# Decoder layer on one core: a piece of the weight maximum placed between VectorE's reciprocal and the context scaling

## The reference

```python
def bitlinear(x, w):
    xq = _act_quant(_rmsnorm(x))
    wq = _weight_quant(w)
    return jnp.einsum('bsd,ed->bse', xq, wq)
...
scores = jnp.einsum('bshd,bstd->bsht', q, k) / Dh ** 0.5
attn = jax.nn.softmax(scores, axis=-1)
ctx = jnp.einsum('bsht,bstd->bshd', attn, v)
ctx = jnp.swapaxes(ctx, 1, 2).reshape(B, S, D)
return bitlinear(ctx, wo)
...
o = jnp.einsum('bsef,edf->bsed', h, W2) + b2
```

## Time and profile before

| | us |
|---|---|
| median of 3 runs | 783.32 (782.77 to 783.34) |
| the profiled execution, its time | 779.51 |
| its span | 777.8 |
| VectorE busy in the span | 573.6 (74%) |
| TensorE busy (matmuls) | 626.6 (81%) |
| ScalarE, GpSimd busy | 488.9, 492.7 (63% each) |
| the loop of self-attention slots | from 67.8 to 215.2 |

### The profile page before, as it was taken

The page is one execution under the profiler, slowest core; times in us unless marked ns, Lnnn a source line. Parts: engine busy times, 40 slices in busy tenths (PEclk is TensorE's granted clock), DMA queues, the critical chain, the costliest instruction groups (busy, mean ns, idle before and its releaser), DMA issues.

```text
span 777.8 us, 20249 instructions
## 1 busy us (share of the span) xinstructions
PE 626.6 (81%) x6601; PEld 544.6 (70%) x6601; DVE 573.6 (74%) x1717; ACT 488.9 (63%) x994; POOL 492.7 (63%) x669
## 2 busy tenths in 40 slices
PE   2588988888898579999999999897789996778600
PEld 0367877777798468888888888786678885666500
DVE  4998988889874676779778797873585664777464
ACT  4675888778835666777777777564445553355514
POOL 6277777877763744636878777644667764666553
PEclk9699999999999689999999999899799998999955
DMA  6611111121125143443110000100223335221241
GB/s 185 182 18 21 22 22 24 20 24 20 20 36 196 79 165 147 174 168 129 34 37 18 30 24 18 56 24 33 76 73 107 101 98 150 59 74 56 66 112 54
DMA packets 115462, 57.40 MB, mean 74 GB/s; under 512 B 70960, under 2 KB 105968, under 8 KB 115376
## 3 DMA queue, kind: packets, MB, share of 16 engines
q1 hardware_dynamic: 105888, 26.49, 15.2%
q10 hardware_dynamic: 4496, 19.02, 6.3%
q0 software_dynamic: 4992, 10.76, 4.0%
HBM read 22.29 MB, written 33.96 MB: 72 GB/s over the span
## 4 chain that ended last, share of the span: by engine, by line
PE 43%; DVE 28%; issue 12%; ACT 7%; POOL 3%; DMA 3%; SPq 1%; DVEq 1%; ACTq 0%; POOLq 0%
PE PS L1176 12%; PE PS L975 5%; DVE PS L1866 5%; PE PS L1086 4%; PE PS L1096 3%; DVE W_raw L2170 2%; PE PS L1262 2%; PE PS L1279 2%; DVE bn L1822 2%; PE PS L1281 2%; PE PS L1280 2%; PE PS L1264 1%; PE PS L1263 1%; DMA W_raw<-in_L_ffn_W_dram 1%; DVE PS L1870 1%
## 5 line engine op out<-in xcount | busy, mean ns | idle before, releaser
L975 PE MATMUL PS<-prod,ident 128*128 128x144 f32 x1024 | 137.3, 294 | 22.0 <-DVE hctx L1846 21.9
L975 PEld LDWEIGHTS PS<-prod,ident 128*128 128x128 f32 x1024 | 131.5, 195 | 30.8 <-issue 24.9
L750 POOL TENSOR_TENSOR prod<-prod,v 128x2048 f32<-128x2048 f32 x32 | 117.5, 3672 | 33.1 <-ACT prod L1373 33.1
L1176 PE MATMUL PS<-W_raw 128*72 128x128 f32 x1024 | 128.1, 280 | 3.1 <-DVE att L2084 1.9
L870 POOL DMA_INDIRECT ys<-W_raw,ids x92 | 91.2, 991 | 60.1 <-ACT W_raw L1605 28.0
L1176 PEld LDWEIGHTS PS<-W_raw 128*72 128x72 f32 x1024 | 114.5, 146 | 8.5 <-issue 5.1
L2063 DVE TENSOR_REDUCE m<-PS 128x8 f32<-128x1024 f32 x64 | 77.9, 1218 | 43.9 <-PE PS L1096 43.9
L2170 DVE SCALAR_TENSOR_TENSOR W_raw<-PS,W_raw 128x512 f16<-128x512 f32 x92 | 60.7, 688 | 51.8 <-ACT W_raw L1595 51.8
L810 POOL DMA_INDIRECT xs<-Y,spot_u x64 | 63.6, 994 | 24.3 <-issue 14.2
L1866 DVE TENSOR_REDUCE PS<-pair_sq 128x128 f32<-128x1024 f32 x64 | 75.1, 1219 | 0.3
L1281 PE MATMUL PS<-W_lo,W_raw 128*128 x368 | 71.6, 223 | 0.0
(11 more groups left out here) (298 smaller groups left out, 1569.0 us busy)
## 6 DMA issues: line engine op xcount, KB each, us to landing
xs<-pad ACTq DMA_DIRECT2D x16, 1152.0 KB, 4.6
Y<-xs SPq DMA_DIRECT2D x46, 144.0 KB
W_raw<-ys SPq DMA_DIRECT2D x16, 256.0 KB, 5.0
W_raw<-in_L_ffn_W_dram SPq DMA_DIRECT2D x1, 2048.0 KB
shuffle<-hctx SPq DMA_DIRECT2D x32, 64.0 KB, 3.0
Y<-shuffle SPq DMA_DIRECT2D x32, 64.0 KB, 1.8
cs<-in_ctx_dram SPq DMA_DIRECT2D x8, 256.0 KB, 2.9
out_dram<-W_raw SPq DMA_DIRECT2D x8, 256.0 KB, 2.3
```

The source lines that it names most:

```text
L750: pool.tensor_tensor(rows[:, :, 0:D].rearrange("p t (d h) -> p t d h", d=HD), a.broadcast_to((P, H, HD, H)), v.broadcast_to((P, H, HD, H)) ...
L975: last = pe.matmul(PS[:, 6, 0:TC], ident[:], prod2[:, i % 2, TC * t:TC * (t + 1)], start=(t == 0), stop=(t == H - 1))
L1176: last = pe.matmul(PS[0:HO, 7, a * P:(a + 1) * P], v_frame[:, i % 2, a, HO * n:HO * (n + 1)], PT[:, i % 2, 8 * a + n, :], start=(n == 0), ...
```

## The change

In the loop slots the part of the maximum of `W2` is no longer the last step of the slot. It is issued in `context`, behind the reciprocal and ahead of the scaling. The scaling's wait for VectorE's own work names the count that the reciprocal reaches, not that of the step behind it. The slots that are written out (0 to 7, and the four behind the loop) are as they were.

```diff
-            def settle(self):
-                self.eng.wait_ge(self.s, self.n + self.turn)
+            def settle(self, n=None):
+                self.eng.wait_ge(self.s, (self.n if n is None else n) + self.turn)
...
-            def context(u, j):
+            def context(u, j, meanwhile=None):
...
                 step(dve.reciprocal(E1inv[:], PS[:, 6, D:TC]))
-                settle()
+                inverted = ch.n
+                if meanwhile:
+                    meanwhile(k)
+                settle(inverted)
                 after_dma(dve, shuffled, k - 5)
                 dve.scalar_tensor_tensor(hctx[:, i % 2, :].rearrange("p (h d) -> p h d", h=H),
...
+            def largest_part(k):
+
+                step(dve.tensor_reduce(w2_top[:, bass.ds(k - 2 * TB, 1)], w2_flat[:, bass.ds(W2_STEP * k - 2 * TB * W2_STEP, W2_PART)],
+                                       AX.X, ALU.max, apply_absolute_value=True))
...
-                    context(u, j)
+                    context(u, j, None if isinstance(u, int) else largest_part)
...
-                if not isinstance(u, int):
-                    step(dve.tensor_reduce(w2_top[:, bass.ds(k - 2 * TB, 1)], w2_flat[:, bass.ds(W2_STEP * k - 2 * TB * W2_STEP, W2_PART)],
-                                           AX.X, ALU.max, apply_absolute_value=True))
```

## The result

The changed kernel took 778.05 us (median of 9 runs, 775.38 to 779.31) against 781.47 us for the kernel before (median of 9, 779.70 to 783.34). The ratio is 0.9948, with an interval from 0.9931 to 0.9965: 0.52% faster. The forecast was 780.9 us and a gain of 0.3%.

What follows compares the result with a forecast made beforehand. No engine is full; the wait ending last at each place bounds the loop. Five batches gain 2.2 us, the first 0.3, in all 2.5, of which 2.4 passes on: 783.32 - 2.4 = 780.9 us, range 779.8 to 783.2.

Steps and rivals of the forecast that it cites:

- What bounds the loop: Loop batches: no engine full; maximum parts of slots 1 and 2 are paid for, those of 0 and 3 hidden.
- What it takes away and adds: Each loop batch: 0.26 us gained in slot 1, 0.23 in slot 2, 0.05 lost in slot 0; net -0.44 us.
- Slot 0's delay: Slot 0 of a batch: the part's register work runs late, delaying the scaling 0.03 to 0.10 us, taken as 0.05.
- The first batch: First loop batch: TensorE limits slot 1's gain to 0.06 us; with slot 2's 0.23, together 0.29 us.
- The gap: Between reciprocal and scaling: the part fits, scaling staying at 0.48 us in slots 1 to 3; a successor could start at 0.42.
- Rival A: Behind the reduce: no overlap, scaling at 0.58 us, delayed 0.10 to 0.11 in slots 0, 2, 3; 782.5 us, chance 0.12.
- Rival B: Scaling's wait: reciprocal's count seen only after the reduce, scaling at 0.74 us or later; 785.7 us, slower, chance 0.06.
- C: Behind the loop: the loop's gain is taken back by granted clock or a wait; 783.3 us, plus or minus 1, chance 0.11.
- D: Loop: no delay in slot 0 and full first-batch gain, 2.9 us in all; 780.4 us or a little below, chance 0.07.
- The time: Whole kernel: 2.4 us gain taken from the 783.32 us median of three runs, giving 780.9 us.

Runs made afterwards that it cites:

- e5: Changed kernel with a second, unread reduce between reciprocal and scaling in each loop slot; run once, 782.12 us.
- e3: Changed kernel with the scaling waiting for VectorE's newest count instead of the reciprocal's; 783.95 us against 779.21 for the kernel before, ratio 1.0052.
- e10: Changed kernel with an extra VectorE reduce of 2350 elements ahead of the loop; 780.69 us against 781.17 for the kernel before, ratio 1.0005.
- e6: Changed kernel with an extra VectorE reduce of 128x2450 elements right behind the loop; 782.65 us against 779.53 for the kernel before, ratio 1.0043.
- e7: Kernel before with an extra VectorE reduce of 128x2450 elements right behind the loop; 784.55 us against 779.53 without it, ratio 1.0057.
- e12: Changed kernel with the part between reciprocal and scaling only in slots 0 and 3, last step in 1 and 2; once, 783.93 us beside 781.97.

## Why the prediction was right or wrong

**What bounds the loop: right.** The parts of slots 1 and 2 carry the gain and those of slots 0 and 3 give nothing, which the two halves show apart: -2.89 and +0.41 us.

**What it takes away and adds: right in size.** A batch was to gain 0.26 + 0.23 - 0.05 = 0.44 us; it gained 0.452. Slot 0's delay was 0.07 where I took 0.05. The first batch gained 0.1 instead of 0.3: the reciprocals of slots 1 and 2 were released by TensorE there (74.77 and 80.07), that of slot 0 came right behind a register step of the loop's entry (L457), in all three the part started 0.26 to 0.28 us behind the reciprocal, and each scaling came about 0.1 us late (0.63, 0.61 and 0.60 us behind the reciprocal instead of 0.53, 0.52 and 0.49), where I had 0.05 for two of them and nothing for slot 2. For the loop 2.39 us against 2.5.

**The gap: right in mechanism, mis-sized in room.** The scaling kept its place in slots 1 to 3 since its register work runs beside the reduce. Behind it I saw room for 0.06 us more, with the reduce at the 0.34 us that it takes outside the gap; inside it takes 0.29, and a second part cost 0.13 where 0.2 and more were expected.

**Rival A: wrong.** In slot 2 the reduce itself started 0.08 us ahead of the reciprocal's end (128.55 against 128.63), which the rival excludes. Behind the reduce the scaling of that slot started 0.05 us after its end, which by itself would fit the rival. But in slot 0, where the reduce is late, the scaling started 0.03 us before the reduce had ended in three of the five batches, as in this one (92.86 against 92.54 + 0.35), and in e5 it did so by 0.08 us:

```profile
92.54 0.35 DVE L1911 TENSOR_REDUCE w_top<-W_raw  x1
92.86 0.35 DVE L1849 SCALAR_TENSOR_TENSOR hctx<-PS,c_v,E1inv 128x128 f32<-128x128 f32 x1
```

In the other two batches it starts at the reduce's end (116.96 and 116.97), 0.36 us behind the reduce's start, where in slot 0 of e5 the second reduce follows the first by 0.27 (119.76 and 120.03). So slot 0's delay is that of the register work which starts late there, as the prediction had it. The Trainium skill (VectorE: DVE Perf Modes, "The DRAIN you can't avoid") says that the next instruction does not start until the pipe is empty, which I took for this rival, but goes on that one which is not held starts earlier. The rows agree with the second half: e5 shows two neighbouring reduces 0.21 us apart that take 0.29 us each or more.

**Rival B: right as a mechanism, not for this change.** The named count is what keeps it away, as e3 shows.

**Rivals C and D: not what happened.** In the first trace the last stage took back 1.6 us of the loop's 2.4, which looks like C, but in the second trace of the same kernel it did not (46.25 us). D had no delay in slot 0 and a full gain in the first batch; the delay was 0.06 to 0.07 us and the first batch gained 0.13.

**The time: wrong, by the level and by the range.** The step that failed is "I put the difference on the median: 783.32 - 2.4 = 780.9", and with it the range. Three runs of the kernel before lay within 0.6 us of each other, 3.8 above the profiled execution, and I took their agreement for the kernel's level. Nine runs gave a median of 781.47, and later ones of the same program lie between 775.1 and 784.8. A gain of 2.4 us from 781.47 is 779.1, which is already below the range. The range had terms for the delays and none for this. What is left, 1.0 us of medians, is not told from scatter: the ratio of 0.9948 would be 0.9969 for the loop alone, just outside its interval (0.9965), while the repetition gave 0.9976, with 0.9969 well inside. That the change does a little more behind the loop is not excluded; no trace shows it, and e10's interval excludes more than some 2 us (0.9984 is -1.2 us, where the shift is +0.9), if a shift passes on one for one, which e6 and e7 put in doubt.

## What to carry to other kernels

Where an instruction waits for its neighbour on the same engine, look at what fills the gap: here 0.2 of 0.25 us were register instructions of a hardware loop, and independent work of 0.29 us fitted in at no cost where its own register instructions had run ahead (0.06 us where they had not), if the wait names the producer's count and not the newest. Move into such a gap the work that stands on the path; work that is hidden behind another engine's wait gains nothing there and may delay what follows it.

When the effect sought is 0.3%, compare stages between traces, not the ends, and take the level and its scatter from many runs: a few that agree may only be neighbours.

## What the runs showed of the hardware

The same reduce takes 0.34 us at the end of a slot (0.31 in slot 2) and 0.28 to 0.29 us directly behind the reciprocal where it starts before the reciprocal's end; behind a reciprocal that had been waited for it takes 0.35. With two of them in the gap, 0.29 and 0.33 in slot 1. The register instructions for its address, 0.10 us and more, cost nothing in the first case.

The same program with the same inputs took 558.8 us behind the loop in one trace and 563.8 in another. Of that 2.9 us lay in one stretch of some 30 us with sparse matmuls, where the granted clock was 0.87 and 0.83 in the mean, and 1.7 us in the last one, where VectorE's additions wait for rows from DRAM. There one VectorE addition (`W_raw<-W_raw,X`, 128x512), 0.69 us elsewhere, took 1.81 us in the slower trace, at the same time as an addition of GpSimd:

```profile
744.83 0.69 DVE L2183 TENSOR_TENSOR W_raw<-W_raw 128x512 f32<-128x512 f32 x1 [0.39 <-DMA W_raw<-ys]
745.56 1.81 DVE L2185 TENSOR_TENSOR W_raw<-W_raw,X 128x512 f32<-128x512 f32 x1
745.56 1.25 POOL L881 TENSOR_TENSOR X<-X,bet 128x512 f32<-128x512 f32 x1
```

The same happened in e3 (1.84 us) and e12 (1.72 us). In these three of the 14 traces GpSimd's addition starts within 0.1 us of VectorE's, and each time VectorE's ends 0.55 us behind GpSimd's end. In ten others the two do not overlap, and VectorE's takes 0.69 us. In e5 VectorE's starts 0.17 us ahead of GpSimd's; it takes 0.69 us as ever, and GpSimd's 1.65 instead of 1.25. So the two do not go on side by side: one waits for the other, and the start in the rows does not always tell which (in e3 GpSimd's comes 0.04 us after VectorE's, and VectorE's is the one held). What they share is not shown.
